# One read-back transfer per attention stack and half, and one transfer for a group's shift rows

## The reference, cut to what matters

```
q = (x @ wq + bq).reshape(Bb, T, H, hd).transpose(0, 2, 1, 3)
k = (x @ wk + bk).reshape(Bb, T, H, hd).transpose(0, 2, 1, 3)
att = jnp.einsum('bhqd,bhkd->bhqk', q, k) * hd ** (-0.5)
att = jnp.where(causal, att, -jnp.inf)
att = jax.nn.softmax(att, axis=-1)
y = jnp.einsum('bhqk,bhkd->bhqd', att, v)
```

## Time and profile before

| | us |
|---|---|
| median of 3 executions | 3047.06 |
| lowest, highest | 3043.91, 3050.0 |
| profiled execution, its own time | 3046.33 |
| its span in the trace | 3044.6 |
| PE busy, share of the span | 87% |
| DVE busy | 85% |
| DMA, mean | 39 GB/s |

### The profile page before, as it was taken

One profiled execution on the slowest core, in us unless ns is written; L12 is line 12 of the kernel. 1 busy time (PEld: TensorE's weight loads), 2 busy tenths in 40 slices (PEclk: granted clock), 3 DMA queues, 4 the chain that ended last, 5 costly groups with the idle time before them and its releaser, 6 DMA issues. The chain is left out here.

```text
span 3044.6 us, 71512 instructions
## 1 busy us (share of the span) xinstructions
PE 2646.6 (87%) x28144; PEld 1160.3 (38%) x28144; DVE 2598.8 (85%) x3528; ACT 2249.2 (74%) x4330; POOL 637.5 (21%) x1177
## 2 busy tenths in 40 slices
PE   3679999899799995689999999589999898899976
PEld 3432333677323334322222222232334775333325
DVE  4789998787899985799999999598997887899976
ACT  1258988676589884369999999378887675688874
POOL 5233211544321011100000000132102433321011
PEclk8779999999799997889999999799999998899998
DMA  1141000224300000410000000510001223300001
GB/s 34 53 101 39 27 23 16 73 56 97 71 27 16 18 9 24 116 27 11 17 9 17 9 16 9 138 33 29 15 13 34 66 66 89 65 28 16 13 16 28
DMA packets 109883, 119.09 MB, mean 39 GB/s; under 512 B 20726, under 2 KB 87660, under 8 KB 109548
## 3 DMA queue, kind: packets, MB, share of 16 engines
q1 hardware_dynamic: 102444, 98.21, 12.2%
q0 software_dynamic: 4608, 13.96, 2.2%
q10 hardware_dynamic: 2496, 2.36, 0.3%
HBM read 70.31 MB, written 43.78 MB: 37 GB/s over the span
## 5 line engine op out<-in xcount | busy, mean ns | idle before, releaser
L1804 ACT ACTIVATE h_probsg<-h_ps_lowg 128x512 f32<-128x512 f32 (+3 forms) x812 | 424.5, 551 | 108.5 <-PE h_ps_lowg L1734 70.7
L1804 ACT ACTIVATE h_probsf<-h_ps_lowf 128x512 f32<-128x512 f32 (+3 forms) x812 | 424.4, 550 | 107.3 <-PE h_ps_lowf L1734 68.5
L1804 ACT ACTIVATE h_probsb<-h_ps_lowb 128x512 f32<-128x512 f32 x683 | 389.2, 596 | 61.0 <-PE h_ps_lowb L1734 46.2
L1755 PE MATMUL h_ps_valuesg<-h_probsg,v_all 128*9 128x256 f32 (+2 forms) x4608 | 350.2, 376 | 25.9 <-POOL h_probsg L1917 19.0
L1755 PE MATMUL h_ps_valuesf<-h_probsf,v_all 128*9 128x256 f32 (+2 forms) x4608 | 349.0, 375 | 26.0 <-POOL h_probsf L1917 19.3
L1755 PE MATMUL h_ps_valuesb<-h_probsb,v_all 128*9 128x256 f32 x4096 | 317.9, 382 | 7.9 <-ACT h_drainedb L1813 3.1
L1856 DVE TENSOR_REDUCE h_maxima_0b<-h_ps_scanb 128x2 f32<-128x1024 f32 x256 | 292.5, 1213 | 6.7 <-PE h_ps_scanb L1696 6.7
L1856 DVE TENSOR_REDUCE h_maxima_2b<-h_ps_scanb 128x2 f32<-128x1024 f32 x256 | 292.6, 1214 | 5.1 <-PE h_ps_scanb L1696 5.1
L1856 DVE TENSOR_REDUCE h_maxima_0g<-h_ps_scang 128x2 f32<-128x1024 f32 x224 | 258.9, 1216 | 19.8 <-PE h_ps_scang L1696 19.1
L1856 DVE TENSOR_REDUCE h_maxima_0f<-h_ps_scanf 128x2 f32<-128x1024 f32 x224 | 258.6, 1216 | 18.6 <-PE h_ps_scanf L1696 18.0
L1804 ACT ACTIVATE h_probsf<-h_ps_highf 128x512 f32<-128x512 f32 (+3 forms) x404 | 224.0, 554 | 35.0 <-PE h_ps_lowf L1734 32.3
(11 more groups left out here) (465 smaller groups left out, 5240.6 us busy)
## 6 DMA issues: line engine op xcount, KB each, us to landing
q_stack<-combine_weights SPq DMA_DIRECT2D x64, 256.0 KB, 3.7
q_stack<-in_L_ffn_e_w SPq DMA_DIRECT2D x24, 256.0 KB, 3.3
q_stack<-q_parts SPq DMA_DIRECT2D x22, 256.0 KB, 5.5
k_stack<-k_parts SPq DMA_DIRECT2D x22, 256.0 KB, 7.4
attended<-h_drainedf SPq DMA_DIRECT2D x16, 256.0 KB, 2.3
attended<-h_drainedf SPq DMA_DIRECT2D x32, 128.0 KB, 2.0
attended<-h_drainedb SPq DMA_DIRECT2D x32, 128.0 KB, 1.9
attended<-h_drainedg SPq DMA_DIRECT2D x16, 256.0 KB, 2.3
```

The source lines that it names most:

```text
L1755: last = nc.tensor.matmul(ps_values[32 * j:32 * j + VD, low:high], m.v_all[:, kb, QUAD * quad + j, :], probs[:, (u + j % banks) % RING_P, ...
L1804: nc.scalar.activation(by_head(probs[:, of % RING_P, :], of), by_head(ps_scores[of % RING_S], of), ACT.Exp, scale=SOFTMAX_SCALE).then_inc( ...
```

## The change

The slots are reordered so that both six-slot stacks can be read as overlapping windows of the four slots in DRAM: q lies as high, high, mid, low and is read as three runs of two slots (0-1, 1-2, 2-3), k lies as low, high, mid, high and is read as two runs of three slots (0-2, 1-3). The six pairs that are multiplied are the same, in another order. Each stack and half is then read by one transfer of 384 KB, and each read-back semaphore counts 16 a layer instead of 32. The DRAM side of the new transfer has one level more: 3 (q) or 2 (k) runs, each of 128 (q) or 192 (k) pieces of 1 KB. Groups of four tiles write their shift rows for both halves in one transfer, from 16 partitions to partitions 48 and 112. The same edit of `load_stacks` stands at both projections and in `EarlyProjection.load`.

```diff
-Q_SLOTS = [0, 1, 2, 0]
-K_SLOTS = [2, 1, 0, 0]
+Q_SLOTS = [0, 0, 1, 2]
+K_SLOTS = [2, 0, 1, 0]
 SLOTS = len(Q_SLOTS)
-Q_AGAIN, K_AGAIN = 0, 1
-AGAIN = 2
-STACK = (SLOTS + AGAIN) * HD
+Q_RUNS, K_RUNS = (3, 2), (2, 3)
+STACK = 6 * HD
...
+def stack_rows(dram, runs, b, cols):
+
+    first = dram.rearrange("r (hp b) s -> r b hp s", b=2)[0:1, b, 0:1, cols]
+    count, places = runs
+    return bass.AP(first.tensor, first.offset, [[HD * HEADS * S, count], [HEADS * S, places * HD], [2 * S, PAIRS], [1, CH]])
...
                 queue.wait_ge(written[k][c % 2], 16 * 3 * (c // 2 + 1))
                 if c == CHUNKS - 1:
                     queue.wait_ge(v_ready, CHUNKS)
-                at = HALF * b
-                for n, first in ((SLOTS, 0), (AGAIN, again)):
-                    queue.dma_start(stack[at:at + n * HD, c, :, :],
-                                    dram.rearrange("r (hp b) s -> r b hp s", b=2)[first * HD:(first + n) * HD, b, :, cols])\
-                        .then_inc(arrived[b][c], 16)
-                    at += n * HD
+                queue.dma_start(stack[HALF * b:HALF * b + STACK, c, :, :], stack_rows(dram, runs, b, cols))\
+                    .then_inc(arrived[b][c], 16)
...
-        shift_moves.append((2 if tiles == TPC else 4) + (shift_moves[g - 2] if g >= 2 else 0))
-    arrived = 32 * (m.layers + 1)
+        shift_moves.append((1 if tiles == TPC else 4) + (shift_moves[g - 2] if g >= 2 else 0))
+    arrived = 16 * (m.layers + 1)
...
                 sp.wait_ge(freed, plan.turn_at[g] + 1)
+                if n == TPC:
+                    rows = slice(SHIFT_ROW, SHIFT_ROW + HALF + 1, HALF)
+                    sp.dma_start(m.q_stack[rows, c, 2 * quad:2 * quad + 2, :], shifts[0:4 * n, g % 2, :])\
+                        .then_inc(shift_in[g % 2], 16)
                 for b in range(2):
                     row = HALF * b + SHIFT_ROW
-                    if n == TPC:
-                        sp.dma_start(m.q_stack[row:row + 1, c, 2 * quad:2 * quad + 2, :],
-                                     shifts[2 * n * b:2 * n * (b + 1), g % 2, :]).then_inc(shift_in[g % 2], 16)
-                    else:
+                    if n < TPC:
```

More of the change, by code:

```diff
@@ L682, in load_stacks @@
             cols = slice(c * CH, (c + 1) * CH)
-            for k, (stack, dram, arrived, again) in enumerate(((m.q_stack, m.q_dram, m.q_in, Q_AGAIN),
-                                                               (m.k_stack, m.k_dram, m.k_in, K_AGAIN))):
+            for k, (stack, dram, arrived, runs) in enumerate(((m.q_stack, m.q_dram, m.q_in, Q_RUNS),
+                                                               (m.k_stack, m.k_dram, m.k_in, K_RUNS))):
                 queue.wait_ge(written[k][c % 2], 16 * 3 * (c // 2 + 1))
```

## The result

The changed kernel takes 3248.6 us (median of 4 runs, 3242.9 to 3250.5) against 3047.0: ratio 1.0659, 95% interval 1.064 to 1.0677, about 201 us slower. The profiled execution took 3242.9 us, its span is 196.6 us longer than that of before.

The account below looks back on a forecast made before the run. PE, busy 87% of the span, was taken as the bound, with transfers mattering only at the five attention starts. Stalls of 32 + 45 + 18 + 25 + 25 = 145 us on 3046.3 gave 3191 (likeliest 3190), range 3080 to 3380.

Parts of the forecast that it names:

- likeliest case: Narrow reads at 41 to 58 ns a packet: 3110 to 3260 us, likeliest 3190, chance 0.60.
- The number of engines: New reads go over 3 engines (q) and 2 (k), the number dividing both outer counts; ACT's queue would show 2319 packets.
- The rival of a read that is not narrow: Each read stays at 24 packets per engine, nothing stalls, 3 to 8 us saved: 3041 us, chance 0.13.
- The price of a packet: One engine moves a 1 KB packet in 50 ns, with 41 and 77 as ends; each ns is worth 7.4 us.
- f1: Causal layer: four reads ahead make combine weights 8 us late, group 4's scores come 17 us late; +25 us.
- f0: Causal layer: narrow reads delay the first shifts, group 2's scores 39 us late, less 7 given back; +32 us.
- b: Layer whose first two groups need k of all chunks: first shift at 1358 instead of 1313; +45 us.
- The shared engines: SP's and ACT's narrow reads were assumed to use the same first engines: 640 packets, 32 us for f0's chunk 0.
- mostly covered: Rival: ACT's transfers and the second of each pair get other engines than SP's; 84 us less, 3107 us, chance 0.10.
- The give-back: While PE waits for a shift the search runs on, returning 7 us in f0 and 5 in g0.
- g0: Causal layer: group 2's scores move from 1988.7 to 2012, less 5 for the search ahead; +18 us.
- g1: Causal layer with the same code and distances as f1; +25 us.

Follow-up runs that it names:

- Reading later: The changed kernel with SP's narrow reads of chunks 2 and 3 in causal attentions issued behind the shifts of groups 4 and 6: 3181.8 us, ratio 1.0443.
- POOL's order: The changed kernel with two POOL lines swapped in g0's projection, powers before the read of chunk 1: 3241.5 us, ratio 1.0649.
- wide windows: The changed kernel with each run a transfer of its own, three of 16 rows for q, two of 24 for k: 3057.4 us, ratio 1.0045.
- six slots: The changed kernel with six slots in DRAM, so one 384 KB read per stack and half begins with 48 rows: 3052.4 us, ratio 1.0023.

## Why the prediction was right, and where its sum was off

The direction, the mechanism and the range held: 3190 with 3080 to 3380 against 3248.6. The likeliest case's own range, 3110 to 3260, holds it too. By size the sum was short: 145 us against 196.2 in the profile. That a price of 58 ns would have given 3250 is luck: neither price measured is 58, and the sum is off in other terms too.

- **The number of engines** (3 and 2) was right, to the packet: 2319. The rival of a read that is not narrow fell with it.
- **The price of a packet**, 50 ns, is a mean of two prices. With SP's and ACT's reads alone it is 43: in the experts before f1 the four reads hold SP's queue from 749.0 to 776.6 us, 27.6 us for 640 packets, where I had 32. With POOL's narrow reads beside them it is near 57: in f0 the read of chunk 1 holds it from 171.6 to 189.7, 18.1 us for 320 packets, where I had 16. I had entered zero for POOL's reads. In b the reads of chunks 2 and 3 are issued from 1397.0 on and PE's last wait for k ends at 1438.3: 41.3 us for 640 packets, 65 ns, with POOL's reads beside them. The rows of the first case, with the first combine weights behind them:

```profile
749.00 0.79 SPq L1247 DMA_DIRECT2D q_stack<-q_parts  x1
749.83 3.64 SPq L1247 DMA_DIRECT2D k_stack<-k_parts  x1
753.51 8.98 SPq L1247 DMA_DIRECT2D q_stack<-q_parts  x1
762.54 6.03 SPq L1247 DMA_DIRECT2D k_stack<-k_parts  x1
768.62 8.02 SPq L2708 DMA_DIRECT2D q_stack<-combine_weights  x1
```

- **The shared engines** were assumed; the two levels of 73 and 48 GB/s show them, and the rival "mostly covered" fell.
- **The give-back** of 7 us in f0 and 5 in g0, because the search would run on while PE waits for a shift, is the step that failed. The order of PE's work is written out (`plan.tensor`), so a wait for scores holds the search behind it as well. Between the first search and the first scores PE executes the same 98 matmuls in both kernels, busy for the same 8.64 us, and what is longer is only the wait.
- **The clock** has no term in the sum. Group 2's scores in f0 are 44.4 us late, the layer's end 48.9, and the 4.5 us between are no wait: PE's busy time for the same 4227 matmuls is 4.6 us longer, at a granted clock of 0.97 for 0.99. These are rows of the windows view (start and end; length; busy us of PE, PEld, DVE, ACT and POOL; granted clock; DMA share; GB/s), before and then after:

```profile
156.78:172.20 15.42, 8.64 (x98) 4.97 (x99) 12.12 (x13) 0.00 (x0) 2.20 (x4) 0.50 1.06 239
190.40:537.50 347.10, 322.90 (x4227) 108.90 (x4227) 316.47 (x347) 295.92 (x602) 83.25 (x196) 0.99 0.09 26
```

```profile
176.18:199.74 23.56, 8.64 (x98) 4.96 (x99) 12.12 (x13) 0.00 (x0) 2.98 (x2) 0.50 0.44 135
234.84:586.40 351.56, 327.54 (x4227) 109.03 (x4227) 316.18 (x346) 295.86 (x601) 83.20 (x194) 0.97 0.08 26
```

  Over the whole span PE's busy time grew by 15.0 us, which bounds what PE's own slower work can have cost; how much of it was on the path elsewhere no run here shows.
- **f0** (48.9 for 32): first search at 176.2 for 181, first scores at 199.7 for 196, group 2's at 234.8 for 229. The first reads took less than forecast and the later ones more, with the writes that pile up behind a standing queue: from 189.7 to 194.5 they are issued one by one before the shift. Of the 16.9 us missed, 7 are the give-back, 5.4 the later scores of group 2 and 4.5 PE's slower work behind them.
- **g0** (36.7 for 18) was the largest miss. Chunk 1's read occupies SP until 2110.1, and the shift goes out at 2118.6 behind ten writes, where I had let it land with the read. In SP's timeline of g0:

```profile
2088.98 0.71 SPq L957 DMA_DIRECT2D q_stack<-q_parts  x1
...
2091.66 18.41 SPq L946 DMA_DIRECT2D q_parts<-p_partsg  x1
...
2118.56 0.55 SPq L1921 DMA_DIRECT2D q_stack<-h_shiftsg  x1
2119.15 0.72 SPq L957 DMA_DIRECT2D q_stack<-q_parts  x1
...
2125.43 11.55 SPq L1921 DMA_DIRECT2D q_stack<-h_shiftsg  x1
```

  The read of chunk 3 then has to wait until the queue is free of chunk 2's, and group 2's scores come at 2157.3:

```profile
2157.32 0.60 PE L1728 MATMUL h_ps_highg<-q_stack,k_stack 49*128 49x512 bf16 x1 [3.64 <-DMA q_stack<-h_shiftsg]
```

  g0 starts 132.1 us behind the kernel before (the sum of the table's first three), so these scores are 36.5 us late by themselves, for 23.3 in the forecast before its give-back. Of these 13.2 us, 9.0 lie between the end of chunk 1's read and the issue of chunk 2's (2110.1 to 2119.2), where the writes are; the rest is in the length of the reads of chunks 2 and 3. The give-back of 5 completes the miss. Reading later takes back 18 us of g0's loss, POOL's order 3.6.
- **f1** (30.1 for 25) and **g1** (27.5 for 25) are near for a part that is luck: two errors of opposite sign. By SP's first shift, at 841.4 where it was at 777.6, f1 has lost 14.9 us of its own, for 8 in the forecast, and the attention behind it adds 15.2 for 17. In g1 it is 13.2 and 14.3. The four reads held the queue for less time than forecast, but POOL's use of the late weights came at 788.5, 12.0 us late for the 8, just behind the issues of POOL's own reads of chunk 1, which are narrow too.
- **b** (53.1 for 45) has the right mechanism; all of its loss lies before the first shift, at 1445.1 where it was at 1313.0, and the 8 us that are missing fit the dearer packets beside POOL's reads, though no run parts them. PE's waits are where they were said to be, at each next chunk of k:

```profile
1395.95 1.04 PE L1690 MATMUL h_ps_scanb<-k_stack,q_stack 48*128 48x512 bf16 x4 [11.51 <-DMA k_stack<-k_parts]
...
1424.72 1.03 PE L1690 MATMUL h_ps_scanb<-k_stack,q_stack 48*128 48x512 bf16 x4 [20.57 <-DMA k_stack<-k_parts]
...
1438.30 1.04 PE L1690 MATMUL h_ps_scanb<-k_stack,q_stack 48*128 48x512 bf16 x4 [5.38 <-DMA k_stack<-k_parts]
```

- **What is saved**, at most 3 us by the shift transfer: the run with it alone has 2 us at best estimate, with an interval that reaches past zero. (The 0.65 us for an issue is that of b's and f1's rows; the row that was cited has 0.72. Nothing hangs on it.)
- **The rates** in the starts were forecast below 80 GB/s; that holds where only SP and ACT read (59 GB/s from 150 to 160 us), and not with POOL's reads and the part writes beside them (198 from 190 to 200).

## What to carry to other kernels

Before two transfers are merged, look at the outermost count of both patterns as they go into the instruction: a window of 3 or 2 overlapping runs outside turned a 16-engine transfer into one over 3 or 2, and the 80 reads saved cost 201 us. Completion packets in the row of SP's or ACT's queue tell the width exactly. Packets on the busiest engine times 43 ns give how long a queue stands when nothing else reads; beside other narrow reads it was 57 to 65 ns, and the kernel lost a third more than the sum over its queue said. A late transfer costs more than its own length when program orders are written out: what is issued behind it waits, and an engine that waits for it does not go on with its other work.

## What was not expected of the hardware

- The issue of a transfer stood for 16 us on SP's queue while narrow transfers were ahead of it, and for 7.2 us within a pair; issues of 0.4 to 0.6 us are the rule in the kernel before.
- POOL's narrow reads add small packets: its queue has 20448 packets for 4608 before, with 0.26 MB more, about 16 bytes for each added one. Under "under 512 B" the page counts 34643. With k wide and q narrow its queue has 11088 packets, with q wide and k narrow 14688, and with both as wide windows 5328.
- No view lists packets by size, but the trace holds the sizes: on POOL's queue 16320 packets of 16 bytes, 6720 with only q narrow, 10080 with only k narrow, 480 with wide windows, and none with six slots or before. POOL's data packets there are of 4 KB, so a narrow q read is 32 on each of 3 engines and a narrow k read 48 on each of 2. The counts come out to the packet if every engine without data gets as many small packets as the others get of data: 13 x 32 = 416 for q, 14 x 48 = 672 for k, fifteen of each in the changed kernel, and 4 x 4 = 16 for a k window over 12 engines. So a narrow transfer of POOL's occupies all sixteen engines a little, and one over 16 engines has none of these packets. What they cost no run here parts. Its completions do not tell the width: by the same count they are 16 a transfer, narrow or not (4608 + 16320 less 480 for the 30 transfers that are no longer issued is 20448).
